# First tile's queries loaded with features on partitions and centred on TensorE, with its values and keys loaded in halves in another order

## Chip, cores and metric

One Trainium2 chip, one core. The metric is the device time of one launch in microseconds, the median of several runs. The profile shows one execution.

## What is computed

Eight batches of 256 tokens with 256 features. One cross-attention without projections, then a gated feed-forward net with three products of hidden width 1,024, each after a layer norm without weights:

```python
scores = einsum('bqd,bkd->bqk', layernorm(x), ctx) * scale      # scale = 256 ** -0.5
scores = where(causal or key_pad, -inf, scores)
x = x + einsum('bqk,bkd->bqd', softmax(scores), ctx)
n = layernorm(x)
h = silu(tlin(n, w1_w, w1_s)) * tlin(n, w2_w, w2_s)              # tlin: ternary weights, a scale per output
h = gelu(tlin(h, h1_w, h1_s)); h = gelu(tlin(h, h2_w, h2_s))
out = x + tlin(h, w3_w, w3_s)
```

The mean of a query's features is subtracted before the scores; its reciprocal deviation is applied in the exponential, as the scale of the argument.

## The kernel before

The tokens are worked in four tiles of 512: two batches of 256, or four row blocks of 128 (`r` = 0 to 3, batch `b = r // 2`). All is written out by hand: each engine has a list of instructions in a fixed order and waits on semaphores. Tile 0 has functions of its own (`first_...`) for its attention, since nothing else can run beside it; the attention of tiles 1 to 3 is laid between the hidden products of the tile before. From the first gate product (L997) on, TensorE works through gate and up, two hidden layers (L1025) and down (L1044), tile after tile.

Values are held as a high and a low part for the net (`xn_hi`, `xn_lo`), so each weight block is multiplied twice. The weights come from DRAM into `weights`; the first six pieces go raw into tiles that are used otherwise (`raw_pieces`: `gate`, `residual`, `ctx_cols`, `work`, `turned`, `ctx_rows`), each when its tile is free. ACT sums their low bits (`test_piece`, L466); TensorE adds such sums up (`sum_flag`, L1063), DVE makes a flag, and TensorE branches on it (`segment`) before it begins a part of the net.

Attention of tile 0 before the change, for each row block:

1. SP loads the rows of `x` (`load_queries`, L246, one load per batch), the keys with features on partitions (`load_keys`, L250, one per batch), then, after the first rows are in, all values (`load_values`, L256), raw pieces 0 and 1, a staging copy, and the scales. Raw piece 2 is loaded after the last score of tile 0, piece 3 after the last transpose of probabilities, pieces 4 and 5 after the last attention product.
2. DVE makes the statistics (L727, L732), POOL the reciprocal deviation (L402 to L418).
3. ACT (for r = 3: DVE) subtracts the mean from the rows (`first_deviation`, L483, L737).
4. TensorE transposes them (`first_turn`, L1143), and ACT or DVE copies them from PSUM, times the scale, into `q_cols` (`first_queries`, L490, L744).
5. TensorE adds the mask by small bf16 products (`first_mask_in`, L1151, L1153) and the scores onto it (`first_score`, L1161: 128 columns for even r, 256 for odd r, two float32 products each).
6. DVE takes the maximum (L751, L758), ACT the exponential (L497), TensorE transposes the probabilities (L1170), ACT or DVE copies them out (L504, L766), TensorE multiplies them with the values (`first_attend`, L1180), DVE divides, adds `x` (L779) and makes the statistics of the second norm.
7. DVE normalises (L791), TensorE transposes (L1188), ACT and DVE split into high and low part (L510, L798), and the gate products begin.

TensorE's list starts with fillers, products of zeros (`stay_busy`, L1134): 18 before the first transpose, 9 more after the last transpose of probabilities, some single ones later. The functions with the profile's line numbers:

Of the kernel before, what the change touches and what calls it, by code (L numbers as in the profile page):

```python
# [32 lines left out]
EC = EMB // P  # L33
# [3 lines left out]
SCALE = float(EMB) ** -0.5  # L37
# [21 lines left out]
def xattn_ffn(nc, x, x_cols_d, ctx_rows_d, ctx_cols_d, mask_d, weights_d, scales_d, down_scale_d, out):  # L59
# [7 lines left out]
    with stack:  # L67
# [3 lines left out]
        def sem(name):  # L71
            return stack.enter_context(nc.semaphore(name))
# [47 lines left out]
        first_tri = test_out[:, 640:640 + P]  # L120
        first_ident = test_out[:, 768:768 + P]
        xn_first = act32[:, 0:2].rearrange("p n (r d) -> p (n r) d", d=EMB)

        raw_pieces = [gate[:].rearrange("p n t -> p (n t)"), residual[:].rearrange("p r d -> p (r d)"),
                      ctx_cols[:].rearrange("p b c t -> p (b c t)"), work[:], turned[:],
# [11 lines left out]


        first_bank = [ring[0], ring[1], att[0], att[1]]
        first_turn_bank = [ring[3], ring[2], ring[3], ring[2]]  # L140

        staged = [sem(f"staged{n}") for n in range(PIECES // 2)]
        pair_loaded = [sem(f"loaded{n}") for n in range(PIECES // 2)]
# [49 lines left out]
        first_stats = sem("first_stats")  # L193
        first_moments = sem("first_moments")
        first_rstd = sem("first_rstd")
        first_dev = [sem(f"first_dev{r}") for r in range(ROWS)]
        first_turned = sem("first_turned")
        first_q = [sem(f"first_q{r}") for r in range(ROWS)]
        first_scores = [sem(f"first_scores{r}") for r in range(ROWS)]
        first_maxed = sem("first_maxed")  # L200
        first_neg = [sem(f"first_neg{r}") for r in range(ROWS)]
# [27 lines left out]
        def probs_cols(r):  # L229

            return slice(0, P) if r % 2 == 0 else slice(P, KEYS)
# [9 lines left out]
        def _(sp):  # L241
            def load_queries(t):

                for b in range(PAIR):
                    rows = slice(2 * b, 2 * b + 2)
                    sp.dma_start(x_in[:, rows], x[t, b]).then_inc(x_loaded[b], 16)  # L246

            def load_keys(t):
                for b in range(PAIR):
                    sp.dma_start(ctx_cols[:, b], ctx_cols_d[t, b]).then_inc(ctx_cols_in[b], 16)  # L250
# [4 lines left out]
            def load_values(t):  # L255
                sp.dma_start(ctx_rows[:], ctx_rows_d[t]).then_inc(ctx_rows_in, 16)  # L256
# [53 lines left out]
            def load_raw(n):  # L310
                sp.dma_start(raw_pieces[n], weights_d[n]).then_inc(raw_in[n], 16)

            load_queries(0)
            load_keys(0)
            sp.wait_ge(x_loaded[0], 16)
            load_values(0)
            load_raw(0)
            load_raw(1)
            stage(RAW)
# [139 lines left out]
        def _(act):  # L459
# [17 lines left out]
                act.dma_start(work[:, 0:TOK], means_d[t].rearrange("p r -> (p r)").partition_broadcast(P)  # L477
                              ).then_inc(mean_loaded, 16)

            def first_deviation(r):  # L480

                act.wait_ge(first_moments, r + 1)
                nc.scalar.activation(xn[:, r], x_in[:, r], ACT.Identity, bias=mean_var[:, r, 0:1], scale=-1.0  # L483
                                     ).then_inc(first_dev[r], 1)

            def first_queries(r):

                act.wait_ge(first_turned, r + 1)
                b, q = divmod(r, 2)
                nc.scalar.activation(q_cols[:, b, :, q * P:(q + 1) * P],  # L490
                                     first_turn_bank[r][:, 0:EMB].rearrange("p (c t) -> p c t", c=EC), ACT.Copy,
                                     scale=-SCALE).then_inc(first_q[r], 1)

            def first_exponentials(r):

                act.wait_ge(first_neg[r], 1)
                nc.scalar.activation(probs[:, r // 2, probs_cols(r)], first_bank[r][:, 0:(r % 2 + 1) * P], ACT.Exp, bias=neg_max[:, r:r + 1], scale=rstd[:, r:r + 1],  # L497
                                     accum_out=row_sum[:, r:r + 1]).then_inc(first_probs[r], 1)

            def first_evacuate_probs(r):  # L500

                act.wait_ge(first_probs_turned[r], 1)
                cols = probs_cols(r)
                nc.scalar.activation(probs_t[:, r // 2, cols], first_bank[r][:, cols], ACT.Copy  # L504
                                     ).then_inc(first_probs_t[r], 1)
# [87 lines left out]
            act.dma_start(mask[0:1, :, 0:SEQ].bitcast(I32), mask_d[0:1]).then_inc(mask_loaded, 16)  # L593
            act.wait_ge(down_free, ROWS)
            load_table(0, ACT.Exp)
            first_deviation(0)
            first_deviation(1)
            first_queries(0)
            first_deviation(2)
            first_queries(1)  # L600
            first_queries(2)
            first_exponentials(0)
            first_exponentials(1)
            first_exponentials(2)
            first_evacuate_probs(1)
            first_evacuate_probs(2)
            first_exponentials(3)
            test_piece(0)
# [23 lines left out]
        def _(dve):  # L632
# [96 lines left out]
            def first_moments_of(r, norm):  # L729

                dve.wait_ge(first_stats, ROWS * norm + r + 1)
                nc.vector.bn_aggr(out=mean_var[:, r], in_=stats[:, r]).then_inc(first_moments, 1)  # L732

            def first_deviation(r):

                dve.wait_ge(first_moments, r + 1)
                nc.vector.tensor_scalar(xn[:, r], x_in[:, r], mean_var[:, r, 0:1], -1.0, ALU.subtract, ALU.mult  # L737
                                        ).then_inc(first_dev[r], 1)

            def first_queries(r):  # L740

                dve.wait_ge(first_turned, r + 1)
                b, q = divmod(r, 2)
                nc.vector.tensor_scalar(q_cols[:, b, :, q * P:(q + 1) * P],  # L744
                                        first_turn_bank[r][:, 0:EMB].rearrange("p (c t) -> p c t", c=EC), -SCALE, None,
                                        ALU.mult).then_inc(first_q[r], 1)

            def first_max(r):

# [144 lines left out]

            nc.vector.memset(h_lo[0][:, 0, 0:SEQ].bitcast(F32), 0.0).then_inc(idle_made, 1)
            nc.vector.memset(zero_col[:], 0.0).then_inc(down_free, ROWS)
            dve.wait_ge(x_loaded[0], 16)
            first_stats_of(0, x_in)
            first_moments_of(0, 0)
# [4 lines left out]
            first_moments_of(2, 0)  # L904
            first_stats_of(3, x_in)
            first_moments_of(3, 0)
            first_deviation(3)
            first_max(0)
            first_neg_max(0)
            first_queries(3)  # L910
            first_max(1)
            first_neg_max(1)
            first_evacuate_probs(0)
# [35 lines left out]
        def _(pe):  # L949
# [11 lines left out]

            def attend(t, b):
                if b == 0:
                    pe.wait_ge(ctx_rows_in, 16 * (t + 1))
# [172 lines left out]
            def first_turn(r):  # L1137

                pe.wait_ge(first_dev[r], 1)
                if r >= 2:  # L1140
                    pe.wait_ge(first_q[r - 2], 1)
                for c in range(EC):
                    ins = nc.tensor.transpose(first_turn_bank[r][:, c * P:(c + 1) * P], xn[:, r, c * P:(c + 1) * P], ident[:])  # L1143
                ins.then_inc(first_turned, 1)

            def first_mask_in(b):

# [7 lines left out]
            def first_score(r):  # L1155

                b, q = divmod(r, 2)
                pe.wait_ge(ctx_cols_in[b], 16)
                pe.wait_ge(first_q[r], 1)
                for c in range(EC):  # L1160
                    ins = nc.tensor.matmul(first_bank[r][:, 0:(q + 1) * P], q_cols[:, b, c, q * P:(q + 1) * P],  # L1161
                                           ctx_cols[:, b, c, 0:(q + 1) * P], start=False, stop=(c == EC - 1))
                ins.then_inc(first_scores[r], 1)
# [9 lines left out]
            def first_attend(r):  # L1173

                b, q = divmod(r, 2)
                cols = probs_cols(r)
                pe.wait_ge(first_probs_t[r], 1)
                for k in range(q + 1):
                    at = cols.start + k * P
                    ins = nc.tensor.matmul(first_bank[r][:, 0:EMB], probs_t[:, b, at:at + P], ctx_rows[:, 2 * b + k],  # L1180
                                           start=(k == 0), stop=(k == q))
                ins.then_inc(first_attended[r], 1)
# [7 lines left out]
                ins.then_inc(first_xn_turned[r], 1)  # L1190

            pe.wait_ge(idle_made, 1)
            stay_busy(18)
            pe.wait_ge(ident_made, 1)
            pe.wait_ge(first_consts, 3)
            first_turn(0)
            first_mask_in(0)
            first_turn(1)
            first_score(0)
            first_turn(2)  # L1200
            first_turn(3)
            first_score(1)
            first_mask_in(1)
            first_turn_probs(0)
            first_score(2)
            first_score(3)
            first_turn_probs(1)
            pe.wait_ge(ctx_rows_in, 16)
            first_attend(0)
            first_turn_probs(2)  # L1210
            first_attend(1)
            first_attend(2)
            first_turn_probs(3)
            stay_busy(9)
# [45 lines left out]
```

## Time and profile before

| | us |
|---|---|
| median of 3 runs | 363.42 (362.03 to 363.5) |
| the profiled execution, its own time | 363.59 |
| its span in the trace | 361.8 |
| start of the first gate product in it | 17.14 |

Engines: TensorE is busy for 356.6 us of the span, DVE for 181.8, ACT for 147.6, POOL for 35.8. Times in views count from the span's start. The chain of waits is followed back from the last instruction; each of its pieces lasts from the end of the one before it to its own end, so that its starts lie a little behind those of the timeline. A float32 matrix product is recorded as two matmul instructions, a transpose or a product of another type as one.

### The profile page before, as it was taken

Reading aid. Unit: us, or ns where it says so; the run is one execution under the profiler, and the core shown is the slowest. Engines: PE = TensorE matmul, PEld = TensorE weight load, DVE = VectorE, ACT = ScalarE, POOL = GpSimd, SP = SyncE. Lnnn points to the kernel's source line nnn. Section 1 sums busy time; section 2 is a strip of 40 time slices with the busy share of each in tenths; the row PEclk is TensorE's granted clock in tenths of the full one; section 3 lists DMA queues with packets and bytes.
Section 4 is the critical chain, followed back from the end, with each engine's and each line's share of the span. In section 5 each row is a group of like instructions: output and inputs, shape, how many; then the busy total and the mean of one; then the engine's idle time right before and its main releaser. Section 6 shows DMA issues by size and latency. Waiting matters only on the chain.

```text
span 361.8 us, 4628 instructions
## 1 busy us (share of the span) xinstructions
PE 356.6 (99%) x1746; PEld 300.9 (83%) x1746; DVE 181.8 (50%) x402; ACT 147.6 (41%) x247; POOL 35.8 (10%) x59
## 2 busy tenths in 40 slices
PE   8999999999999999999999999999999999999996
PEld 7888787888898888888898888888889888888886
DVE  3859326435648764338345845335626662323233
ACT  4789953761136622521143641621123652212120
POOL 7450103100100220001000050001000000000000
PEclk9999999999999999999999999999999999999999
DMA  7799989969269000210833010030411000000001
GB/s 253 276 380 416 408 316 377 432 153 356 59 136 350 12 29 0 67 22 11 206 108 112 3 29 0 21 68 0 94 23 47 14 1 0 2 0 0 2 0 62
DMA packets 39569, 43.82 MB, mean 121 GB/s; under 512 B 23746, under 2 KB 32068, under 8 KB 39364
## 3 DMA queue, kind: packets, MB, share of 16 engines
q1 hardware_dynamic: 38672, 42.62, 35.2%
q10 hardware_dynamic: 868, 0.80, 0.8%
q8 instruction: 20, 0.33, 0.4%
q14 instruction: 9, 0.07, 0.1%
HBM read 38.55 MB, written 16.39 MB: 152 GB/s over the span
## 4 chain that ended last, share of the span: by engine, by line
PE 98%; DVE 0%; ACT 0%; issue 0%
PE ring L1025 65%; PE ring L997 16%; PE ring L1044 8%; PE att L957 2%; PE att L969 2%; PE ring L1134 2%; PE ring L1180 0%; PE ring L1143 0%; PE att L1161 0%; PE ring L1161 0%; ACT act L569 0%; PE ring L1188 0%; PE att L1188 0%; PE att L1063 0%; PE ring L1151 0%
## 5 line engine op out<-in xcount | busy, mean ns | idle before, releaser
L1025 PE MATMUL ring<-h_hi,weights 128*128 128x512 f32 x512 | 201.2, 393 | 0.8 <-ACT act L569 0.8
L1025 PE MATMUL ring<-h_lo,weights 128*128 128x512 f32 x512 | 199.6, 390 | 0.0
L1025 PEld LDWEIGHTS ring<-h_hi,weights 128*128 128x128 f32 x512 | 96.1, 188 | 22.0 <-ACT act L569 1.2
L1025 PEld LDWEIGHTS ring<-h_lo,weights 128*128 128x128 f32 x512 | 96.2, 188 | 19.7
L569 ACT ACTIVATE act<-ring,scales 128x512 f32<-128x512 f32 x64 | 44.1, 688 | 155.7 <-PE ring L1025 155.5
L838 DVE CAST h_hi<-act 128x512 fp32r<-128x512 f32 x64 | 27.5, 429 | 123.1 <-ACT act L569 123.0
L722 DVE TENSOR_TENSOR h_lo<-act,h_hi 128x512 fp32r<-128x512 f32 x96 | 66.5, 693 | 2.3
L997 PE MATMUL ring<-xn_hi,weights 128*128 128x512 f32 (+1 forms) x140 | 51.6, 375 | 0.2 <-DVE xn_lo L798 0.2
L997 PE MATMUL ring<-xn_lo,weights 128*128 128x512 f32 (+1 forms) x140 | 51.2, 372 | 0.0
L549 ACT ACTIVATE gate<-ring,scales 128x512 f32<-128x512 f32 x32 | 22.0, 688 | 26.3 <-PE ring L997 26.3
L1044 PE MATMUL ring<-weights,h_lo 128*128 128x256 f32 x128 | 30.9, 283 | 0.0
L1044 PE MATMUL ring<-weights,h_hi 128*128 128x256 f32 x128 | 30.9, 283 | 0.0
L997 PEld LDWEIGHTS ring<-xn_hi,weights 128*128 128x128 f32 x140 | 26.3, 188 | 5.3 <-POOL weights L436 0.5
L997 PEld LDWEIGHTS ring<-xn_lo,weights 128*128 128x128 f32 x140 | 26.4, 189 | 4.4
L819 DVE SCALAR_TENSOR_TENSOR act<-ring,scales,gate 128x512 f32<-128x512 f32 x32 | 24.0, 749 | 12.0 <-PE ring L997 9.9
L1044 PEld LDWEIGHTS ring<-weights,h_lo 128*128 128x128 f32 x128 | 24.6, 192 | 0.2
L1044 PEld LDWEIGHTS ring<-weights,h_hi 128*128 128x128 f32 x128 | 24.5, 192 | 0.2
L539 ACT ACTIVATE h_hi<-act 128x512 fp32r<-128x512 f32 x32 | 20.0, 626 | 2.0 <-DVE act L819 2.0
L466 ACT ACTIVATE scaled<-weights 128x1024 bf16<-128x1024 uint16 x16 | 16.8, 1053 | 3.6 <-DMA weights<-weights_staged 2.9
L402 POOL TENSOR_SCALAR var_eps<-mean_var 128x4 f32<-128x4 f32 (+2 forms) x12 | 2.4, 199 | 104.4 <-DVE mean_var L647 101.6
L851 DVE TENSOR_TENSOR scaled<-ring,down_scale 128x256 f32<-128x256 f32 x16 | 6.8, 422 | 7.3 <-PE ring L1044 7.3
L569 ACT ACT_TABLE_LOAD x7 | 9.0, 1283 | 2.7 <-POOL mean_scaled L409 2.6
(125 smaller groups left out, 215.2 us busy)
## 6 DMA issues: line engine op xcount, KB each, us to landing
weights<-weights_staged SPq DMA_DIRECT2D x11, 1024.0 KB, 8.8
x_in<-in_x SPq DMA_DIRECT2D x8, 256.0 KB, 4.6
ctx_cols<-in_ctx_cols SPq DMA_DIRECT2D x8, 256.0 KB, 5.4
ctx_rows<-in_ctx_rows SPq DMA_DIRECT2D x4, 512.0 KB, 6.9
out_dram<-residual SPq DMA_DIRECT2D x16, 128.0 KB, 2.0
turned<-in_x_cols SPq DMA_DIRECT2D x3, 512.0 KB, 8.4
xn_blocks<-work SPq DMA_DIRECT2D x3, 512.0 KB, 3.2
turned<-xn_blocks SPq DMA_DIRECT2D x12, 128.0 KB, 2.8
```

The source lines that it names most:

```text
L466: nc.scalar.activation(test_out, low, ACT.Copy, accum_out=low_sums[:, n:n + 1]).then_inc(low_summed, 1)
L539: nc.scalar.activation(h_hi[0][:, c], act32[:, c % 3], ACT.Copy).then_inc(hi_done, 1)
L549: nc.scalar.activation(gate[:, c % 2], ring[2 * c % RING][:], ACT.Silu, scale=gate_scale[:, c:c + 1]).then_inc(gate_done, 1)
L569: nc.scalar.activation(act32[:, n % 3], ring[(2 * HC + HC * layer + c) % RING][:], ACT.Gelu, scale=scale[:, c:c + 1]).then_inc(gelu_done, 1)
L722: nc.vector.tensor_tensor(h_lo[buf][:, c], act32[:, n % 3], h_hi[buf][:, c].bitcast(F32), op=ALU.subtract).then_inc(split, 1)
L819: nc.vector.scalar_tensor_tensor(out=act32[:, c % 3], in0=ring[(2 * c + 1) % RING][:], scalar=up_scale[:, c:c + 1], in1=gate[:, c % 2], op ...
L838: nc.vector.tensor_copy(h_hi[buf][:, c], act32[:, n % 3]).then_inc(hi_made, 1)
L957: ins = nc.tensor.matmul(att[b][:, cols], q_cols[:, b, c, q * P:(q + 1) * P], ctx_cols[:, b, c, 0:(q + 1) * P], start=(c == 0), stop=(c == ...
L969: ins = nc.tensor.matmul(att[b][:, q * EMB:(q + 1) * EMB], later_probs_t[:, b, n * P:(n + 1) * P], ctx_rows[:, 2 * b + k], start=(k == 0), ...
L997: ins = nc.tensor.matmul(bank[:, toks], w, part[:, k, toks].bitcast(dt), start=(k == 0 and part is xn_hi), stop=(k == EC - 1 and part is x ...
L1025: ins = nc.tensor.matmul(bank[:], w, part[:, k].bitcast(dt), start=(k == 0 and part is h_hi[src]), stop=(k == HC - 1 and part is h_lo[src]))
L1044: ins = nc.tensor.matmul(bank[:, 0:EMB], part[:, k, r * P:(r + 1) * P].bitcast(dt), w, start=(k == 0 and part is h_hi[0]), stop=(k == last ...
```

## The change

Tile 0 alone is changed. The queries are loaded a second time, with features on partitions (`first_cols`, in `act32`), and the mean is taken off by a product: for each half of the features `c`, the sum over both halves `k` of a 128x128 matrix times the queries. The matrix is -SCALE/256 everywhere (`minus_mean`) and has SCALE added on its diagonal where `k` is `c` (`own_minus_mean`); DVE makes both in `x_attn`. ACT copies each result (`first_queries(b, c)`) into `q_cols`. The rows of `x` are still loaded, for the statistics and the sum after the attention. SP's loads, TensorE's and ACT's lists are in a new order:

```diff
-            load_queries(0)
-            load_keys(0)
+            load_first_rows(0)
+            load_first_cols(0)
+            load_first_keys(0)
+            load_first_rows(1)
+            load_first_cols(1)
             sp.wait_ge(x_loaded[0], 16)
-            load_values(0)
+            load_first_values(0)
+            load_first_keys(1)
+            load_first_values(1)
             load_raw(0)
...
-            first_deviation(0)
-            first_deviation(1)
-            first_queries(0)
-            first_deviation(2)
-            first_queries(1)
-            first_queries(2)
+            first_queries(0, 0)
+            first_queries(0, 1)
             first_exponentials(0)
+            first_queries(1, 0)
             first_exponentials(1)
+            first_queries(1, 1)
+            first_evacuate_probs(1)
             first_exponentials(2)
-            first_evacuate_probs(1)
             first_evacuate_probs(2)
             first_exponentials(3)
...
+            nc.vector.memset(minus_mean, -SCALE / EMB).then_inc(minus_mean_made, 1)
+            dve.wait_ge(ident_made, 1)
+            dve.wait_ge(minus_mean_made, 1)
+            nc.vector.scalar_tensor_tensor(out=own_minus_mean, in0=ident[:], scalar=SCALE, in1=minus_mean,
+                                           op0=ALU.mult, op1=ALU.add).then_inc(own_minus_mean_made, 1)
             dve.wait_ge(x_loaded[0], 16)
...
-            first_deviation(3)
             first_max(0)
             first_neg_max(0)
-            first_queries(3)
...
+            def first_centre(b, c):
+
+                pe.wait_ge(first_cols_in[b], 16)
+                if b == 1:
+                    pe.wait_ge(first_q[0], c + 1)
+                for k in range(EC):
+                    ins = nc.tensor.matmul(first_centre_bank[c][:, 0:SEQ], own_minus_mean if k == c else minus_mean,
+                                           first_cols[:, b, k], start=(k == 0), stop=(k == EC - 1))
+                ins.then_inc(first_centred, 1)
...
                 pe.wait_ge(ctx_cols_in[b], 16)
-                pe.wait_ge(first_q[r], 1)
+                pe.wait_ge(first_q[b], EC)
...
+                pe.wait_ge(first_values_in[b], 16)
                 pe.wait_ge(first_probs_t[r], 1)
...
-            stay_busy(18)
+            stay_busy(14)
+            pe.wait_ge(own_minus_mean_made, 1)
+            first_centre(0, 0)
+            first_centre(0, 1)
             pe.wait_ge(ident_made, 1)
             pe.wait_ge(first_consts, 3)
-            first_turn(0)
             first_mask_in(0)
-            first_turn(1)
             first_score(0)
-            first_turn(2)
-            first_turn(3)
             first_score(1)
+            first_centre(1, 0)
+            first_turn_probs(0)
             first_mask_in(1)
-            first_turn_probs(0)
+            first_centre(1, 1)
+            first_turn_probs(1)
+            first_attend(0)
             first_score(2)
             first_score(3)
-            first_turn_probs(1)
-            pe.wait_ge(ctx_rows_in, 16)
-            first_attend(0)
+            first_attend(1)
             first_turn_probs(2)
-            first_attend(1)
             first_attend(2)
             first_turn_probs(3)
             stay_busy(9)
```

`load_first_rows(b)`, `load_first_cols(b)` and `load_first_keys(b)` load 256 KB each, as does `load_first_values(b)`, two of the four row blocks. All are 128 runs of 2 KB.

## Rows read from the trace of the kernel before

**Rows 1.** The page: busy time, the chain by engine, the costliest group
```profile
PE 356.6 (99%) x1746; PEld 300.9 (83%) x1746; DVE 181.8 (50%) x402; ACT 147.6 (41%) x247; POOL 35.8 (10%) x59
...
PE 98%; DVE 0%; ACT 0%; issue 0%
...
L1025 PE MATMUL ring<-h_hi,weights 128*128 128x512 f32 x512 | 201.2, 393 | 0.8 <-ACT act L569 0.8
```

**Rows 2.** Chain of waits, 0 to 17.4 us: start us, us, engine, tile, line
```profile
1.17 4.21 PE ring L1134 x18
...
5.38 0.42 PE ring L1143 x2
...
6.78 0.40 PE ring L1143 x2
7.18 0.45 PE ring L1161 x4
7.63 0.53 PE ring L1143 x4
8.15 0.86 PE ring L1161 x4
9.02 0.21 PE att L1151
...
9.71 0.11 PE ring L1170
9.83 1.31 PE att L1161 x8
11.14 0.22 PE ring L1170 x2
11.36 0.43 PE ring L1180 x2
...
13.61 1.07 PE ring L1134 x9
...
17.14 0.36 PE ring L997
```

**Rows 3.** Chain of waits, a stretch at 3 us
```profile
2.82 0.85 PE ring L1134 x4
```

**Rows 4.** Busy time and granted clock by stretch
```profile
1.17:5.18 4.01, 4.01 (x19) 4.01 (x20) 1.69 (x7) 2.50 (x4) 3.43 (x11) 1.00 0.80 216
...
7.00:13.37 6.37, 6.37 (x40) 4.97 (x39) 4.37 (x15) 4.25 (x13) 2.44 (x7) 1.00 0.99 379
```

**Rows 5.** Timeline of ACT: start us, us, line, operation, out<-in
```profile
11.94 0.28 ACT L504 ACTIVATE turned<-att 128x128 f32<-128x128 f32 x1 [0.16 <-PE att L1170]
12.11 0.56 ACT L497 ACTIVATE work<-att,neg_max,rstd 128x256 f32<-128x256 f32 x1
...
13.96 1.06 ACT L466 ACTIVATE scaled<-residual 128x1024 bf16<-128x1024 uint16 x1
...
15.12 0.38 ACT L510 ACTIVATE xn_hi<-ring 128x256 fp32r<-128x256 f32 x1
```

**Rows 6.** Timeline of DVE at the last scores
```profile
11.18 0.42 DVE L751 TENSOR_REDUCE row_max<-att 128x1 f32<-128x256 f32 x1 [0.29 <-PE att L1161]
...
11.83 0.48 DVE L779 SCALAR_TENSOR_TENSOR x_attn<-ring,inv_sum,x_in 128x256 f32<-128x256 f32 x1
```

**Rows 7.** Timeline of DVE at the first statistics
```profile
3.39 0.43 DVE L727 BATCH_NORM_STATS2 stats<-x_in 128x6 f32<-128x256 f32 x1 [2.27 <-DMA x_in<-in_x]
...
4.48 0.39 DVE L727 BATCH_NORM_STATS2 stats<-x_in 128x6 f32<-128x256 f32 x1
```

**Rows 8.** Timeline of POOL, its copy of weight piece 0
```profile
10.85 1.03 POOL L436 CAST weights<-gate 128x1024 fp32r<-128x1024 f32 x1 [2.40 <-DMA gate<-in_weights]
```

**Rows 9.** Timeline of SP, the two key loads
```profile
1.62 1.02 SPq L250 DMA_DIRECT2D ctx_cols<-in_ctx_cols  x2
```

**Rows 10.** DMA issues, 0 to 5 us: KB each, median us to landing
```profile
ctx_cols<-in_ctx_cols SPq DMA_DIRECT2D x2, 256.0 KB, 4.2
```

More of the change, by code:

```diff
@@ L122, in xattn_ffn @@
         xn_first = act32[:, 0:2].rearrange("p n (r d) -> p (n r) d", d=EMB)
+        first_cols = act32[:, 0:2].rearrange("p b (c t) -> p b c t", c=EC)
+        minus_mean = x_attn[:, 0, 0:P]
+        own_minus_mean = x_attn[:, 0, P:2 * P]
         raw_pieces = [gate[:].rearrange("p n t -> p (n t)"), residual[:].rearrange("p r d -> p (r d)"),
@@ L139, in xattn_ffn @@
         first_bank = [ring[0], ring[1], att[0], att[1]]
-        first_turn_bank = [ring[3], ring[2], ring[3], ring[2]]
+        first_centre_bank = [ring[3], ring[2]]
         staged = [sem(f"staged{n}") for n in range(PIECES // 2)]
@@ L195, in xattn_ffn @@
         first_rstd = sem("first_rstd")
-        first_dev = [sem(f"first_dev{r}") for r in range(ROWS)]
-        first_turned = sem("first_turned")
-        first_q = [sem(f"first_q{r}") for r in range(ROWS)]
+        first_cols_in = [sem(f"first_cols_in{b}") for b in range(PAIR)]
+        first_values_in = [sem(f"first_values_in{b}") for b in range(PAIR)]
+        minus_mean_made = sem("minus_mean_made")
+        own_minus_mean_made = sem("own_minus_mean_made")
+        first_centred = sem("first_centred")
+        first_q = [sem(f"first_q{b}") for b in range(PAIR)]
         first_scores = [sem(f"first_scores{r}") for r in range(ROWS)]
@@ L311, in load_raw, with load_first_rows, load_first_cols, load_first_keys @@
                 sp.dma_start(raw_pieces[n], weights_d[n]).then_inc(raw_in[n], 16)
-            load_queries(0)
-            load_keys(0)
+            def load_first_rows(b):
+                sp.dma_start(x_in[:, 2 * b:2 * b + 2], x[0, b]).then_inc(x_loaded[b], 16)
+            def load_first_cols(b):
+                sp.dma_start(first_cols[:, b], x_cols_d[0, b]).then_inc(first_cols_in[b], 16)
+            def load_first_keys(b):
+                sp.dma_start(ctx_cols[:, b], ctx_cols_d[0, b]).then_inc(ctx_cols_in[b], 16)
+            def load_first_values(b):
+                rows = slice(2 * b, 2 * b + 2)
+                sp.dma_start(ctx_rows[:, rows], ctx_rows_d[0][:, rows]).then_inc(first_values_in[b], 16)
+            load_first_rows(0)
[3 more added lines that the diff above has]
+            load_first_cols(1)
             sp.wait_ge(x_loaded[0], 16)
-            load_values(0)
+            load_first_values(0)
+            load_first_keys(1)
+            load_first_values(1)
             load_raw(0)
@@ L478, in spread_means, with first_queries @@
                               ).then_inc(mean_loaded, 16)
[L480 to L492, printed above, removed]
+            def first_queries(b, c):
+                act.wait_ge(first_centred, EC * b + c + 1)
+                nc.scalar.activation(q_cols[:, b, c], first_centre_bank[c][:, 0:SEQ], ACT.Copy
+                                     ).then_inc(first_q[b], 1)
             def first_exponentials(r):
@@ L732, in first_moments_of @@
                 nc.vector.bn_aggr(out=mean_var[:, r], in_=stats[:, r]).then_inc(first_moments, 1)
[L734 to L746, printed above, removed]
             def first_max(r):
@@ L963, in attend @@
                 if b == 0:
-                    pe.wait_ge(ctx_rows_in, 16 * (t + 1))
+                    pe.wait_ge(ctx_rows_in, 16 * t)
                 pe.wait_ge(probs_t_in, 16 * BLOCKS * t)
@@ L1135, in stay_busy @@
                                      stop=True)
[L1137 to L1144, printed above, removed]
+            def first_centre(b, c):
[6 more added lines that the diff above has]
+                ins.then_inc(first_centred, 1)
             def first_mask_in(b):
```

## Prediction

> **What bounds the kernel.** I read the page's engine list first: TensorE is busy 99% of the span, and the chain that ended last is TensorE's to 98% [rows 1]. So a change at the start can only shift what follows: it is worth the time by which it moves the first gate product. I then read the chain of waits up to that product, which starts at 17.14 us [rows 2]. It is to be read as a list without holes: from 1.17 to 16.1 us nearly every piece is TensorE's own, each beginning where the last one ended. Filler products, transposes, masks, scores, attention products, filler again. TensorE is thus already the bound of the attention of tile 0 too, and what counts there is the sum of its work in its order, not the wait of any one row.
>
> Next come the prices of its work. A filler product of 128x256 takes 0.85 / 4 = 0.213 us at 3 us [rows 3] and 1.07 / 9 = 0.119 us at 13.6 us [rows 2]. 256 columns in 0.213 us are 1.2 GHz; the later ones go at the 2.4 GHz level. The column of the granted clock reads 1.00 in both stretches [rows 4], so it does not show this rise. The chain does: two 128x128 float32 transposes cost 0.42 and 0.40 us up to 7.18, and four cost 0.53 right after [rows 2]. I put the rise at 7.0 us; TensorE had worked without a hole since 1.17.
>
> **The change, part by part.**
>
> *First filler.* 14 products instead of 18: 4 x 0.213 = 0.85 us less. They end at 5.38 - 0.85 = 4.53 in the chain's reckoning.
>
> *Centring on TensorE.* It replaces four pairs of transposes (0.42 + 0.40 + 0.53 = 1.35 us) by four calls of two float32 products each, 128x128 by 128x256. The score of row block 1 has that shape: two products are "x4" in the trace, four halves, and take 0.86 us, so 0.43 a product and 0.215 a half, at 2.4 GHz [rows 2]. The 128x128 scores at 7.18 (0.45 for two) confirm that half the columns cost half. At 1.2 GHz I take double, 0.86 a product, as transposes and filler double too. Is the data there at 4.53? The feature copy of batch 0 takes the place in the queue of the second half of the rows, which DVE reads at 4.48 with no wait [rows 7]. So batch 0's first call runs from 4.53 to 6.24; of the second's four halves two begin before the clock rises, at 6.24 and 6.67, and two after it: 6.24 + 0.43 + 0.43 + 0.21 + 0.21 = 7.52. Both calls together: 2.99 us. Batch 1's two calls run at full speed: 1.73 us. Total 4.71 us where 1.35 were: +3.36 us.
>
> *Mask products.* Unchanged in number; those of batch 0 (0.98 us between 5.80 and 6.78) now fall after the rise and I give them the 0.69 us of batch 1's: -0.3 us.
>
> *Deviation and copies.* The four deviations leave ACT and DVE, and four copies of 128x256 from PSUM stay four, at the 0.38 us of the like copy at 15.12 [rows 5]. Nothing of it was in the chain, so I count no gain; they were covered by transposes, masks and scores. What is removed as a latency comes back as another: the first score needs both copies of its batch, the second ending at 7.52 + 0.04 + 0.38 = 7.94, under the masks that end at 8.21.
>
> *New order.* Probabilities' transpose of block 1 (0.22) and the attention product of block 0 (0.43) [rows 2] move ahead of the scores of batch 1: +0.65 us for those scores. TensorE by the new order: masks to 8.21, score 0 to 8.66, score 1 to 9.52, centring of batch 1 to 10.38, transpose 10.49, masks 11.18, centring 12.04, transpose 12.26, attention 12.69, score 2 13.14, score 3 to 14.00. Before, score 3 ended at 11.14. The difference, 2.85 us, is -0.85 + 3.36 - 0.30 + 0.65 to rounding.
>
> *Behind score 3.* DVE took its maximum at 11.18 and began the attention sums of block 0 at 11.83 [rows 6]; both queue behind it, so the sums begin at 14.68. ACT's last exponential began at 12.11, just behind the copy of block 2's probabilities at 11.94 [rows 5]. That copy now waits for its transpose, which follows attention block 1 (0.86 us) and ends at 14.00 + 0.86 + 0.11 = 14.97. The exponential starts at 15.17, +3.06 us. Behind it stand in ACT's queue the test of piece 0, a copy, the test of piece 1 (13.96) and the first split at 15.12, back to back [rows 5]. They carry 3.06 us to the flag, to the next transposes and to the first gate product: 20.2 instead of 17.14. The nine fillers at 13.61 stay and absorb nothing, since DVE's chain is 2.85 later as well.
>
> *The added memset and combination on DVE* sit before 3.39, where DVE waited 2.27 us for the rows [rows 7]: nothing, or at most two operations of DVE's 0.43 us if that cover were gone.
>
> *The queue of loads.* 512 KB are added, and SP issues two queries' copies ahead of the values. Landings: first 256 KB at 3.39; rows, keys, values and piece 0, 2,048 KB, by 10.85 [rows 7, 8]. That is 256 KB per 1.07 us, and the second key load, 6.4 us, fits (issued near 2.2, landed 4.2 later [rows 9, 10]). By that rate: rows of batch 1 at 6.6 (before about 4.1), its feature copy 7.7 (needed 9.52), values 0 at 8.7 (needed 12.26), keys 1 at 9.8 (needed 12.69), values 1 at 10.9 (needed after 14), piece 0 at 13.0, piece 1 at 15.1 (tested at 13.96 + 3.06 = 17.0). All covered: nothing. DVE's statistics of batch 1 end near 7.7 (1.09 us for a batch, from 3.39 to 4.48), still before its first maximum at 8.7. If cover went, a load a microsecond late costs that microsecond. POOL's copy of piece 0 (1.03 us) stands ahead of the second norm's reciprocal roots in its queue, but ends at 14.0, before the attention sums even begin. The other raw pieces, behind score 3, are issued as much later as they are used.
>
> *After tile 0's attention* TensorE has one wait of 0.8 us in the whole rest, on ACT [rows 1], and SP's queue starts from the same moment; nothing absorbs the shift but that.
>
> Sum: +3.1 us on the profiled execution's 363.59 (span 361.8 and 1.8 around it) is 366.7. The median of the runs lies 0.17 lower, so I say 366.5.
>
> **A page against the sum.** The rows show one rise, at 7.0 us. The Trainium skill (TensorE: Matmul & The Clock Gate, section "What's actually happening") says that the number of slow products at the start differs from run to run of one kernel. If so, the rise may come before the centring, and the sum would be +1.8 instead of +3.1. The three times of before spread over 1.47 us, which neither proves nor excludes it.
>
> **Rivals.**
> 1. *The clock rises earlier*, by about 2.5 us. Batch 0's centring then costs 1.73, not 2.99: 1.26 less, 365.2. For it: the spread of before. Against: the one trace, in which filler without a hole did not bring it sooner; the new kernel works no denser before 4.5 us.
> 2. *A load comes too late.* The narrowest cover is that of keys 1 and of piece 1's test, 1.9 to 2.9 us. If the 4.2 us of latency grow with seven smaller loads in flight and the landings come 3 to 4 us later than above, score 2 waits about 1 us: 367.6. Against: the loads are of equal size to those in the trace.
> 3. *Not slower: the shorter path to the first scores decides.* Statistics, deviation and transposes no longer stand ahead of the score. If TensorE had holes after the first score to hold batch 1's 1.73 us and the moved 0.65, score 1 would end at 8.3 to 9.0 instead of 9.02, and the time be 362.7 to 363.4. This decides once 2.4 us of holes exist between 7.2 and 13.4 us; the chain shows some tenths.
> 4. *The delay is taken up in part*, by the 0.8 us wait and by fillers that overlap: 2 us or less remain, 364.5 to 365.
>
> **How the numbers follow.** My forecast has 0.68 (own range 365.9 to 367.2, from half a microsecond of transition cost at the clock's rise either way), rival 1 0.13, rival 2 0.07, rival 3 0.05, rival 4 0.07. The range reaches down to rival 1 with 0.2 to spare and up past rival 2: 365.0 to 368.0. Half a per cent is 1.8 us, about what a measurement of this kernel can tell from no change: slower means above 365.2. That holds for the forecast, rival 2 and half of rival 1: 0.84 with a little taken off for spread. Same: rivals 4, half of 1 and most of 3: 0.13. Faster: 0.03.
>
> **What the profile would show.** First centring product near 4.3 us, products of 0.43 us a half at first; score 0 not before 8.2; score 3 ending near 14.0; the last exponential near 15.2; the first gate product near 20.2, and the same span from there to the end as before, 344.7 us. A TensorE wait on a load before 15 us would speak for rival 2, centring halves of 0.22 us from the start for rival 1. The prediction is wrong if the trace shows float32 products of 256 columns cheaper than 0.43 us, or TensorE idle for over a microsecond between 4.5 and 14.

## The result and the profile after

The changed kernel takes 366.16 us, median of 6 runs (365.94 to 367.06); the kernel before took 362.99 in 6 runs (361.86 to 363.97). The ratio is 1.0079, 95% interval 1.0048 to 1.0109: slower, by 2.9 us (1.7 to 4.0). The difference of the two medians is 3.2 us. Forecast were 366.5, in 365.0 to 368.0. The profiled execution took 365.94 us, span 364.1.

The page of the changed kernel: busy time, the chain by engine, and the group of hidden products that answers to the last of [rows 1].

```profile
PE 358.1 (98%) x1750; PEld 301.6 (83%) x1750; DVE 182.6 (50%) x402; ACT 146.3 (40%) x245; POOL 36.1 (10%) x59
...
PE 97%; DMA 1%; ACT 1%; DVE 0%; issue 0%; SPq 0%
...
L1028 PE MATMUL ring<-h_hi,weights 128*128 128x512 f32 x512 | 201.2, 393 | 0.0
```

Its chain of waits up to the first gate product, against [rows 2]; L1146 is the centring, L1165 the scores, L1174 the transposes of probabilities, L1185 the attention products; on ACT, L520 copies probabilities, L513 is the exponential and L490 the test of a weight piece:

```profile
1.16 3.94 DMA act<-in_x_cols
5.10 0.14 issue
5.24 1.97 PE ring L1146 x8
...
7.89 1.42 PE ring L1165 x8
9.31 0.86 PE ring L1146 x4
...
10.98 0.92 PE ring L1146 x4
11.90 0.22 PE ring L1174 x2
12.12 0.43 PE ring L1185 x2
12.55 1.46 PE att L1165 x8
14.01 0.86 PE ring L1185 x4
...
15.02 0.28 ACT turned L520
15.30 0.55 ACT work L513 x2
15.85 1.04 ACT scaled L490 x2
...
17.04 1.16 ACT scaled L490 x2
...
20.20 1.91 PE ring L1000 x14
```

From 5.24 to 15.0 us the chain is TensorE's without a break again, and longer by the centring. Behind it ACT's list carries the delay, as the prediction said. The last score ends at 14.01 us instead of 11.14, the first gate product starts at 20.20 instead of 17.14: 3.06 us. After it the two runs are alike but for one wait. From the first gate product to the start of the last matmul it is 340.54 us in the changed kernel and 341.33 in the kernel before; the difference is a wait of 0.8 us in front of the second hidden layer, which only the trace of the kernel before has. The last stretch, 3.33 us, is the same.

The forecast's timetable is hit at the last score (14.00 said, 14.01 measured), but by errors that cancel. The features of batch 0 land at 5.10 us, so TensorE stands idle for 0.71 us before the centring, which was to start at 4.53. Batch 0's eight halves then take 1.97 us instead of 2.99, at the full clock: the trace's clock record, which marks the rise to the 2.4 GHz level, starts at 4.95 us, where that of the kernel before starts at 7.02. That is 1.02 us less. The other 0.3 us lie in the two groups of scores, 1.42 and 1.46 us where 1.31 was priced, and in the last centring, 0.92 where 0.86 was.

### The profile page after: what moved, and what is told of

The parts are those of the page before. It is cut to its first block, busy times and chain, and to the rows that moved or that the text cites. A ratio compares the mean times of both kernels' runs of the same rounds, so it can differ in the third digit from the quotient of the medians.

```text
span 364.1 us, 4642 instructions
## 1 busy us (share of the span) xinstructions
PE 358.1 (98%) x1750; PEld 301.6 (83%) x1750; DVE 182.6 (50%) x402; ACT 146.3 (40%) x245; POOL 36.1 (10%) x59
## 4 chain that ended last, share of the span: by engine, by line
PE 97%; DMA 1%; ACT 1%; DVE 0%; issue 0%; SPq 0%
PE ring L1028 64%; PE ring L1000 16%; PE ring L1047 8%; PE att L960 2%; PE att L972 2%; DMA act<-in_x_cols 1%; PE ring L1146 1%; ACT scaled L490 1%; PE att L1165 0%; PE ring L1165 0%; PE ring L1185 0%; PE att L1193 0%; PE att L1066 0%; ACT work L513 0%; PE ring L1137 0%
## 5 line engine op out<-in xcount | busy, mean ns | idle before, releaser
L490 ACT ACTIVATE scaled<-weights 128x1024 bf16<-128x1024 uint16 x16 | 16.8, 1052 | 0.8
```

The costliest lines, as they stand in the source:

```text
L490: nc.scalar.activation(test_out, low, ACT.Copy, accum_out=low_sums[:, n:n + 1]).then_inc(low_summed, 1)
```

## Experiments

The expectations below set two theories against each other. Theory 1 is the prediction's: TensorE's work, in its order, is the cost. Theory 2 is that the loads are. The table has twelve more traces beside the first two, read by the same marks, in us. "Rise" is the start of the clock record; "centring" is where TensorE begins it; "last score" is where the last score ends, and "first gate product" where that product starts. The last two columns are the wait in front of the second hidden layer, as the step in TensorE's shift against the changed kernel there (0 stands for 0.13 or less), and the time from the last matmul's start to the end.

| run | rise | centring | last score | first gate product | later wait | end |
|---|---|---|---|---|---|---|
| before | 7.02 | | 11.14 | 17.14 | 0.8 | 3.33 |
| before_again | 5.83 | | 10.71 | 17.14 | 0.5 | 3.33 |
| changed | 4.95 | 5.24 | 14.01 | 20.20 | 0 | 3.33 |
| after_again | 5.29 | 4.32 | 13.56 | 19.71 | 0.6 | 3.34 |
| e1_loads_only | 5.79 | | 11.42 | 17.84 | 0 | 5.43 |
| e2_old_probs_order | 5.38 | 4.33 | 13.55 | 19.78 | 0.8 | 4.73 |
| e3_half_products | 7.17 | 4.33 | 13.02 | 19.17 | 0 | 3.33 |
| e4_masks_first | 9.86 | 5.50 | 16.07 | 22.27 | 0 | 3.33 |
| e5_dead_products | 4.87 | | 12.04 | 18.04 | 0 | 3.33 |
| e6_one_pass | 10.69 | 5.01 | 13.70 | 19.85 | 0 | 3.33 |
| e7_one_pass_filled | 10.82 | 4.96 | 13.68 | 19.83 | 0.3 | 3.33 |
| e8_filled_old_order | 10.70 | 5.13 | 13.76 | 19.82 | 0 | 3.33 |
| e9_later_copy | 6.43 | | 10.91 | 16.91 | 0 | 3.32 |
| e10_later_copy_again | 6.34 | | 10.86 | 16.86 | 1.0 | 4.87 |

Rise, later wait and end all differ between runs of one kernel: the rise in the kernel before (7.02 and 5.83), the later wait and the end in the kernel of e9 and e10 (0 and 1.0, 3.32 and 4.87). Later wait and end together are worth up to some 3 us. So terms under a microsecond are read off the marks, and what only the marks show is said to be so.

**e1: the loads alone, in the kernel before.** The edit also has the waits that the split loads need.

```diff
-            load_queries(0)
-            load_keys(0)
+            load_first_rows(0)
+            load_first_cols(0)
+            load_first_keys(0)
+            load_first_rows(1)
+            load_first_cols(1)
...
-            load_values(0)
+            load_first_values(0)
+            load_first_keys(1)
+            load_first_values(1)
```

> The kernel before with the changed kernel's loads (feature copies of the queries too, which nothing reads) in its order and halves. First gate product: 17.14 us before, 20.20 changed. Theory 1 (TensorE's work in its order is the cost): the loads alone cost only what the later rows of batch 1 (6.8 instead of 4.1 us) do to the deviations, which stand ahead of score 1 on TensorE: first gate product at 17.7 to 17.9, time 0.6 to 0.7 us over before. Theory 2 (the loads are the cost): 19 to 20 us, and +2 to +3 us.

Measured: first gate product at 17.84 us, where theory 1 had it; 364.79 us against 363.61, ratio 1.0021 (0.9996 to 1.0045). Theory 2, with 19 to 20 us, falls. In the chain of this run the rows of batch 1 stand where they did not before, and hold up the deviation and the transposes ahead of score 1:

```profile
2.20 4.15 DMA x_in<-in_x
...
6.37 0.44 DVE stats L748
...
7.05 0.52 ACT work L504
...
7.61 0.82 PE ring L1166 x4
8.43 0.86 PE ring L1184 x4
...
10.92 0.65 DVE neg_max L779
```

The 0.70 us are not all theirs, though. The last score ends only 0.28 us later than in the kernel before (11.42 against 11.14), after a clock that rose 1.2 us sooner. The other 0.42 us appear between the last score and the first gate product, and the chain has their cause: the small DVE operation in the last line takes 0.65 us where it usually takes 0.16, beside a copy of POOL's (both are shown below for the kernel before). So the expectation hit the number, but not for its reason alone. Neither part is a term of the changed kernel in its two traces: it does not need these rows before the first maximum, and POOL's copy meets no such operation there.

**e3: half the centring products.**

```diff
-                for k in range(EC):
-                    ins = nc.tensor.matmul(first_centre_bank[c][:, 0:SEQ], own_minus_mean if k == c else minus_mean,
-                                           first_cols[:, b, k], start=(k == 0), stop=(k == EC - 1))
+                ins = nc.tensor.matmul(first_centre_bank[c][:, 0:SEQ], own_minus_mean, first_cols[:, b, c],
+                                       start=True, stop=True)
```

> The changed kernel without the four products that add the other half of the features to the mean, so that tile 0's queries are not rightly centred; waits and loads as they are. Theory 1: batch 0 and batch 1 each save 2 x 0.43 = 0.86 us at full clock, score 3 ends at 12.3 instead of 14.0, first gate product at 18.4 to 18.6, time 1.6 us under the changed kernel. Theory 2 (loads): unchanged at 20.2.

Measured: last score 13.02, first gate product 19.17 us. Both are 1.0 us before those of the changed kernel's first trace and 0.5 us before those of its second. In the trace the direction is theory 1's and the size short of it. The median shows no gain: 366.29 us, ratio 1.0070 (1.0038 to 1.0102), against the changed kernel's 1.0079; 1.6 us were expected, and these ten runs spread over 4.0 us. So this run supports theory 1 by its marks only. Two reasons for the short size are in the trace. The clock rose at 7.17 us, so batch 0's four halves were slow, 0.43 us apart. And the first maximum now waited for something else: score 0 was done at 7.77, but DVE was still at the statistics of batch 1, whose rows landed at 7.19.

```profile
2.21 4.98 DMA x_in<-in_x
7.22 0.44 DVE stats L741
...
8.30 0.27 DVE row_max L751
...
9.39 0.33 PE ring L1173
```

A load that I had costed as covered lies 0.5 us behind the cover as soon as the centring is shorter.

**e5: TensorE work alone, in the kernel before.**

```diff
             first_score(1)
+            for _ in range(4):
+                nc.tensor.matmul(ring[RING - 1][:, 0:SEQ], ident[:], h_lo[0][:, 0, 0:SEQ].bitcast(F32), start=True,
+                                 stop=True)
             first_mask_in(1)
```

> The kernel before with four more float32 products of 128x256 on zeros behind score 1, read by nobody. They are as much TensorE work as the centring of batch 1. Theory 1: 1.73 us less the holes of some tenths: first gate product at 18.6 to 18.9, time 1.3 to 1.7 us over before. If the latencies of ACT and DVE bound this stretch: below 17.6.

Its chain:

```profile
7.33 0.86 PE ring L1161 x4
8.20 1.73 PE ring L1204 x8
...
10.73 1.31 PE att L1161 x8
12.04 0.22 PE ring L1170 x2
```

The four products (L1204) take 1.73 us, 0.216 a half, and are in the chain in full: from the end of score 1 to that of score 3 it is 3.84 us here and 2.12 before [rows 2]. That TensorE bounds this stretch is shown, and so is the price of a float32 product. The first gate product starts at 18.04, only 0.9 us later than before and below the 18.6 to 18.9 expected. The clock accounts for that: it rose at 4.87, so score 1 was done at 8.20 instead of 9.02, and 1.73 - 0.82 is 0.91. From the last score to the first gate product it is 6.00 us in both. Time: 364.14 us, ratio 1.0029 (1.0000 to 1.0058), about 1.05 us more, where 1.3 to 1.7 were expected.

**e2: the order of the probabilities.**

```diff
             first_queries(1, 1)
+            first_exponentials(2)
             first_evacuate_probs(1)
-            first_exponentials(2)
             first_evacuate_probs(2)
...
             first_centre(1, 1)
+            first_score(2)
+            first_score(3)
             first_turn_probs(1)
             first_attend(0)
-            first_score(2)
-            first_score(3)
+            first_turn_probs(2)
             first_attend(1)
-            first_turn_probs(2)
             first_attend(2)
```

> The changed kernel with the transpose of block 1's probabilities and the attention product of block 0 behind the scores of batch 1 again, on TensorE and with ACT's copy behind the exponential of block 2. Theory 1: score 3 ends 0.65 us earlier (13.35), first gate product at 19.5 to 19.7. If the order is neutral, because the work is only moved: 20.2.

Measured: last score 13.55, first gate product 19.78 us; after_again, the second trace of the changed kernel (below), has almost the same rise and 13.56 and 19.71. So the 0.65 us expected are not there. The chain shows what lies in the freed place:

```profile
10.52 0.93 PE ring L1146 x4
...
11.48 0.39 ACT turned L507
...
12.00 1.55 PE att L1165 x8
```

Score 2 needs ACT's copy of the last centred half, 0.55 us from product to product. In the changed kernel the moved transpose and attention product fill this wait; without them TensorE stands. Time: 366.22 us, ratio 1.0070 (1.0042 to 1.0099).

**Both kernels once more.**

> The kernel before, profiled once more. In the traces so far the cold filler ends where the clock rises, and that was at 7.02, 4.95, 7.17, 5.79, 5.38 and 4.87 us. If the rise is by chance and not by the kernel, it lies elsewhere here too, and the first gate product starts between 16.3 us (rise near 4.9: what four dead products, started with an early rise, leave after taking off their 1.73 us) and 17.2 us (rise at 7.0). The rest of the span is 343.9 us, or 344.7 where the wait of 0.8 us on ACT is there.

> The changed kernel, profiled once more. Theory 1 (TensorE's work): first gate product at 19.7 us with an early rise and the feature copy landed by 4.3 us, at 20.2 to 20.4 with a rise near 7 us. A rival, that 20.20 was set by the late landing of the copy at 5.10 us: 19.7 or less whatever the clock.

Measured: 17.14 and 19.71 us, 363.40 and 365.95 us, one execution each. The changed kernel came where it was expected. In its first trace TensorE began the centring 0.72 us later by the chain (5.24 against 4.52) and took 0.22 us less for it. The difference is the 0.49 us between 20.20 and 19.71, so the late landing made 20.20. Its chain:

```profile
4.52 2.19 PE ring L1146 x8
...
8.83 0.86 PE ring L1146 x4
...
10.53 0.92 PE ring L1146 x4
```

The chain of the kernel before has the transposes in the same place:

```profile
5.38 0.43 PE ring L1143 x2
...
6.53 0.23 PE ring L1143 x2
...
7.20 0.53 PE ring L1143 x4
```

The kernel before did not reach its first gate product sooner with its earlier rise, though its last score ended 0.43 us sooner. Its DVE timeline shows where this went, POOL's beside it:

```profile
10.75 0.42 DVE L751 TENSOR_REDUCE row_max<-att 128x1 f32<-128x256 f32 x1 [0.30 <-PE att L1161]
11.21 0.80 DVE L758 SCALAR_TENSOR_TENSOR neg_max<-row_max,neg_rstd 128x1 f32<-128x1 f32 x1
11.93 0.47 DVE L779 SCALAR_TENSOR_TENSOR x_attn<-ring,inv_sum,x_in 128x256 f32<-128x256 f32 x1
```

```profile
10.97 1.03 POOL L436 CAST weights<-gate 128x1024 fp32r<-128x1024 f32 x1 [2.58 <-DMA gate<-in_weights]
```

An operation of 0.16 us took 0.80 and ended with POOL's copy, at 12.0. Its chain runs through it: from the last score to the first gate product it is 6.43 us here and 6.42 in e1, but 6.00 in the first trace. There the same operation took 0.26 us, and TensorE's own fillers, which end at 14.68, set the next step.

**e4: masks ahead of the centring.**

```diff
+            pe.wait_ge(ident_made, 1)
+            pe.wait_ge(first_consts, 3)
+            first_mask_in(0)
             pe.wait_ge(own_minus_mean_made, 1)
             first_centre(0, 0)
             first_centre(0, 1)
-            pe.wait_ge(ident_made, 1)
-            pe.wait_ge(first_consts, 3)
-            first_mask_in(0)
```

> The changed kernel with batch 0's mask products ahead of its centring instead of behind it. TensorE's sum is the same; ACT's copy of the second centred half (0.42 us) is no longer hidden under the masks. Theory 1: no gain where the copy of features is there at 4.3 us (first gate product 0.4 us later, 20.1 to 20.6), up to 0.6 us gain where it lands late. If the masks' wait and not the sum was the cost: 19.5.

Measured: first gate product 22.27 us, 368.34 us, ratio 1.0116 (1.0050 to 1.0182), from 4 runs. That is much later than either expectation. The chain:

```profile
4.69 0.37 PE ring L1155
...
5.71 3.53 PE ring L1146 x8
9.27 0.39 ACT turned L507
...
9.80 1.58 PE ring L1165 x8
```

The eight halves of batch 0's centring took 3.53 us where after_again has 2.19: all at 1.2 GHz, since the clock record starts at 9.86 us. That is 1.34 of the 2.56 us by which this gate product lies behind the one of after_again. Of the rest, the exposed copy is 0.55 us (from the end of the centring to the first score), as expected. The masks at the lower clock are 0.33, the slower scores 0.16, and a wait for POOL's mask row before the masks 0.17.

**e6 and e7: centring in one pass, then with the hole filled.** DVE rounds the features and the two matrices to the net's type; tile 0's queries are centred from rounded values. The main part of the edit:

```diff
+            def round_cols(b):
+
+                dve.wait_ge(first_cols_in[b], 16)
+                nc.vector.tensor_copy(rounded_cols[:, b], first_cols[:, b]).then_inc(first_rounded[b], 1)
...
-                                           first_cols[:, b, k], start=(k == 0), stop=(k == EC - 1))
+                                           rounded_cols[:, b, k], start=(k == 0), stop=(k == EC - 1))
```

> The changed kernel with the centring products in one pass: DVE rounds the feature copy to the type of the net's products (two casts of 0.43 us), so tile 0's queries are centred from rounded values. A product then costs 0.12 us instead of 0.43. Theory 1: 4 x 2 x 0.31 = 2.5 us less TensorE work, 0.5 us of it lost to the first cast: score 3 at 12.0, first gate product at 18.0 to 18.3, time 0.9 to 1.2 us over the kernel before. Theory 2 (loads and order): 20.

```diff
-            stay_busy(14)
+            stay_busy(17)
```

> The one-pass kernel with 17 fillers instead of 14, so that TensorE has no hole while DVE rounds batch 0's features (that kernel's hole was 4.3 to 5.0 us, and its clock rose at 10.7 us where eight other traces had 4.9 to 7.2). If the hole delays the rise: rise at 8 us or earlier, score 1 done at 8.0 to 9.0 instead of 9.85, first gate product at 18.0 to 18.8. If the late rise was chance: it may fall anywhere between 5 and 11 us again, and the fillers are no help.

Measured: first gate product at 19.85 and 19.83 us; 365.46 us (ratio 1.0057, 1.0020 to 1.0094) and 365.51 us (1.0046, 1.0012 to 1.0080). That is near the 20 of theory 2 and far from the 18.0 to 18.3 of theory 1. The products did become cheap. In e6 the three pieces of centring take 1.19, 0.43 and 0.29 us, 2.06 us less than in after_again. But batch 0's products start 0.49 us later, behind DVE's rounding, and masks and scores take 1.7 us more. The chain of the filled one shows this last part:

```profile
1.17 4.00 PE ring L1148 x17
5.17 0.97 PE ring L1157 x4
...
7.12 2.67 PE ring L1176 x8
9.79 0.43 PE ring L1157 x2
```

Batch 0's scores take 2.67 us for the same eight instructions that took 1.42 in the changed kernel: half rate, with the clock's rise at 10.82 us. The hole before the centring is not its cause, since here TensorE worked without one from 1.17 us on. The first explanation in e7's expectation falls; why the rise was late stays open. So theory 1 is not refuted by these two runs, but its forecast for them failed for want of the clock.

**e8: e7 with e2's order.** The diff is e2's, TensorE's and ACT's, on e7.

> The same with the probabilities of block 1 and the attention product of block 0 behind batch 1's scores again. Theory 1 (TensorE's sum in its order): 0.65 us less up to score 3, first gate product 17.4 to 18.2. This is the changed kernel with each cost that was found taken away but the loads; it should come within 0.3% of the kernel before. Queries of tile 0 are centred from rounded values.

Measured: 19.82 us, 365.62 us, ratio 1.0054 (1.0020 to 1.0089), where 17.4 to 18.2 us and at most 0.3% over the kernel before were expected. The order is worth nothing again, the clock rose at 10.70, and the expectation failed on both.

**e9 and e10: POOL's copy out of DVE's way, in the kernel before.**

```diff
-            first_weights(0)
             first_attention_rstd(0)
             first_attention_rstd(1)
             pool.wait_ge(first_xn[1], 1)
+            first_weights(0)
+            first_attention_rstd(2)
             first_weights(1)
-            first_attention_rstd(2)
             first_attention_rstd(3)
```

> The kernel before with POOL's copies of weight pieces 0 and 1 each one place later in its list, so that the copy of piece 0 (10.85 to 11.88 us, 10.97 to 12.00 in the second trace) no longer runs beside DVE's last row maximum. In both traces DVE's small operation behind that maximum ended with POOL's copy (11.90, 12.01) and took 0.26 and 0.80 us where the others took 0.16. If the copy holds it up: it takes 0.16 us here, the first gate product starts at 16.5 to 16.9 with an early clock rise, 17.0 with a late one. If not: 17.14 as before.

> The kernel with POOL's copies one place later once more, in more rounds, since its median lay 0.18% under the kernel before with an interval that holds no change. The trace gave 0.23 us at the first gate product (16.91 instead of 17.14), 0.06%. If that is all: ratio between 0.998 and 1.001, an interval over 1. The small operation behind the last maximum takes 0.16 us again, and the first gate product lies between 16.5 and 17.0 unless the clock rises after 7.2 us.

DVE's timeline in e9:

```profile
10.95 0.42 DVE L751 TENSOR_REDUCE row_max<-att 128x1 f32<-128x256 f32 x1 [0.29 <-PE att L1161]
11.41 0.16 DVE L758 SCALAR_TENSOR_TENSOR neg_max<-row_max,neg_rstd 128x1 f32<-128x1 f32 x1
11.60 0.48 DVE L779 SCALAR_TENSOR_TENSOR x_attn<-ring,inv_sum,x_in 128x256 f32<-128x256 f32 x1
```

The hold is gone: 0.16 us, and the gate starts at 16.91 and 16.86 us, 6.00 us behind the last score in both. The times are 363.16 and 363.50 us, with ratios of 0.9982 (0.9954 to 1.0011) and 1.0001 (0.9975 to 1.0026): no change that can be told. The chain of e9 shows why even its 0.25 us are lost. POOL's later copies delay the reciprocal roots of blocks 2 and 3, and TensorE waits 0.33 us for the last normalised rows:

```profile
17.37 0.99 POOL weights L436
...
19.37 0.42 DVE act L791
...
19.84 0.33 PE att L1188
```

TensorE's matmuls are 0.36 us behind those of the changed kernel from there on, counted from the first gate product. No version here is faster than the kernel before by more than the noise.

## Why the prediction was right, step by step

- **TensorE bounds tile 0's attention, so its work adds up.** Shown in the traces: e5's 1.73 us of dead products stand in the chain in full, and the changed kernel's chain is TensorE's from 5.24 to 15.0 us. That the loads are not the cost is shown by e1.
- **A float32 product of 128x256 costs 0.43 us at the full clock.** The two calls of batch 1 take 0.86 and 0.92 us, two products each. At 1.2 GHz the price doubles: e4's 3.53 us for eight halves, 0.44 each.
- **Centring adds 3.36 us.** Too much. Between the second traces of the two kernels it is 2.19 + 0.86 + 0.92 = 3.97 us of centring against 0.43 + 0.23 + 0.53 = 1.19 of transposes, so 2.78. The 0.6 us too much are the clock: I took its rise at 7.0 us as the kernel's, and it is the run's. The two traces of each kernel have 7.02 and 5.83, and 4.95 and 5.29. The Trainium skill (TensorE: Matmul & The Clock Gate, section "What's actually happening") says just this, and the traces agree. So rival 1's mechanism came true, by the sign that was set for it: centring halves 0.22 us apart nearly from the start, in the profiled execution. It was not a rival but part of the common case. Its 1.26 us overstates what it does to the ratio, since the kernel before gains from an early rise too, up to where POOL's copy holds it.
- **The masks of batch 0 gain 0.3 us.** Only against a late clock. They take 0.69 us in after_again and 0.72 in before_again. This error and the scores' (about 0.2 us more than priced) offset most of the centring's: between the second traces the last score moves by 2.85 us, which is the prediction's figure by luck.
- **The new order costs 0.65 us.** As a part of the sum up to score 3, yes; as something that the change could have avoided, no (e2, e8). I had looked at what TensorE does and not at the wait that this work fills: the copy of the last centred half.
- **The loads cost nothing.** Nearly. Keys, values and pieces came in time in both traces. The features of batch 0 did so in one (the second trace has no wait for them) and came 0.6 us late in the other (5.10). This wait on a load is the sign set for rival 2, on another load than the one named. The prediction called the cover of keys 1 the narrowest, 1.9 us or more. By its own rate the features of batch 0 land at 3.39 + 1.07 = 4.46 us and are needed at 4.53, a cover of 0.07 us. It did not list them among the covers and went by a read at 4.48 us in the kernel before instead. The same rate put piece 0 at 13.0 us; POOL's copy of it, which waits for the landing, starts at 11.01. e1 and e3 show how thin the cover of batch 1's rows is.
- **Behind the last score: 2.85 us on DVE, 3.06 us on ACT, first gate product at 20.2.** Last score 14.01 (said: 14.00), last exponential 15.20 (15.17), gate 20.20 (20.2). The path is as said: copy of the probabilities, exponential and the two tests stand in ACT's list in the chain. That it fits to hundredths is luck: early clock, late features and dearer scores cancel. The second trace has 13.56, 14.74 and 19.71, a difference of 2.57 us from the kernel before.
- **Nothing absorbs the shift but a wait of 0.8 us.** In the first pair of traces that wait was gone after the change, in the second it was 0.5 and 0.6 us. So it is not the change that takes it away, and rival 4 is not shown. By the first pair of profiled executions the change costs 2.35 us, by the second 2.55, by the ratio 2.9. The span from the first gate product to the end was 343.9 us and not the 344.7 of the forecast, by this wait.
- **Rival 3** (the shorter path to the first scores) has nothing in its favour: score 1 is done at 9.31 and 8.83, where the kernel before has 9.02 and 8.60.
- **The chances.** They do not add up as written: forecast, rival 2 and half of rival 1 are 0.68 + 0.07 + 0.065 = 0.815, not a little over 0.84, which leaves 0.185 and not 0.16 for the rest.

In all, the mechanism was right, and the largest term 0.6 us too large. The size fits as well as it does because the errors of single terms, up to a microsecond, went both ways.

**Open.** Why the clock rose at 9.86 to 10.82 us in e4, e6, e7 and e8, each seen once, when ten other traces have 4.87 to 7.17. All four traces with an edit to the masks' place or to the centring's type are late and none of the ten others. The late ones come from two chips, which gave early ones too. So chance alone is unlikely, though the group was drawn up after the fact; a second trace of any of them is missing. Holes in TensorE's work do not tell them apart: e7 has none up to 9.79 us. The spread of e6's times (363.95 to 367.81) may mean that its rise varies too. It was not settled either what sets the wait before the second hidden layer and the end of 3.3 to 5.4 us.

## What to carry to other kernels

Before moving work to an engine, read the chain for holes: where the receiving engine has none, the work adds its full time, however short the latency that it replaces. List every load with the time at which it is needed, the first one too. Before costing a reordering as pure work, ask which wait the moved piece fills. And with effects of half a per cent, take a second trace of each kernel before pricing a term from one: here the clock's rise moved by 1.2 us between two executions of one kernel, and by over 2 us over ten traces.

## What had not been expected of the hardware

DVE's small operation on two SBUF operands (`neg_max`, L758 in the kernel before, 0.16 us) did not finish beside POOL's copy of 128x1024. It took 0.26, 0.80, 0.64 and 0.97 us in before, before_again, e1 and e4, the four traces where the two met, and ended at 11.90, 12.01, 11.56 and 12.84 us where the copy ended at 11.88, 12.00, 11.54 and 12.82. With the copy moved away, in e9 and e10, it took 0.16 us each time. DVE's row maximum from PSUM was not held (0.42 us beside the same copy, in before from 11.18 to 11.60 us and as long as without it). The Trainium skill (SBUF — State Buffer, section "Terms") calls it a port pair that the two share, where "the loser fully blocks"; this is what the traces show. So in the kernel before, the landing of a weight piece, which starts POOL's copy, can set a floor under the attention of tile 0. In before_again it did, and the earlier clock did not bring the first gate product forward. That both traces have 17.14 us is chance: in the first, TensorE's own list set it.
